# Local attention without the row maximum, with each head's transposed part issued one head later

## The reference

```python
q = q.reshape(Bq * h, nb, window, d) * scale          # window 128, d 64
kk = look_around(k); vv = look_around(v)              # 3 blocks = 384 keys
sim = jnp.einsum('bnid,bnjd->bnij', q, kk)
sim = jnp.where(valid, sim, neg)                      # keys beyond either end of the sequence
attn = jax.nn.softmax(sim, axis=-1)
out = jnp.einsum('bnij,bnjd->bnid', attn, vv)
```

## Time and profile before

| | us |
|---|---|
| median of the two timed runs | 4406.5 (4383.72 and 4429.28) |
| the profiled execution | 4304.85 |
| its span, first to last instruction, slowest core (core 7) | 4303.3 |
| spans of the eight cores | 4293.8 to 4303.3 |
| mean granted TensorE clock of the cores (1 is full speed) | 0.709 to 0.711 |

### The profile page before, as it was taken

One profiled execution on the slowest core, in us unless ns is written; L12 is line 12 of the kernel. 1 busy time (PEld: TensorE's weight loads), 2 busy tenths in 40 slices (PEclk: granted clock), 3 DMA queues, 4 the chain that ended last, 5 costly groups with the idle time before them and its releaser, 6 DMA issues.

```text
span 4303.3 us, 34639 instructions; the slowest of 8 cores (4293.8 to 4303.3 us)
## 1 busy us (share of the span) xinstructions
PE 1987.4 (46%) x10661; PEld 955.0 (22%) x10661; DVE 993.4 (23%) x2186; ACT 898.7 (21%) x1889; POOL 34.9 (1%) x68
## 2 busy tenths in 40 slices
PE   1223455434334333433334678683011566666666
PEld 0011122211111111111112455451001222222222
DVE  2243322122222222222232211212234111011111
ACT  0122322222222222222210222321012111111111
POOL 0000000000000000000011000000000000000000
PEclk9566777655555555555566889896555799999999
DMA  7311111301100100010046110103621000000000
GB/s 236 116 58 60 65 59 54 103 30 44 35 25 30 54 25 25 30 44 25 10 144 195 59 48 30 54 20 95 183 98 59 32 25 13 25 25 25 25 25 10
DMA packets 107777, 249.52 MB, mean 58 GB/s; under 512 B 29865, under 2 KB 44337, under 8 KB 105550
## 3 DMA queue, kind: packets, MB, share of 16 engines
q1 hardware_dynamic: 74544, 170.20, 12.9%
q10 hardware_dynamic: 27938, 60.33, 3.6%
q0 software_dynamic: 5120, 16.78, 1.1%
HBM read 186.95 MB, written 60.32 MB: 57 GB/s over the span
## 4 chain that ended last, share of the span: by engine, by line
PE 41%; DVE 18%; ACT 16%; issue 11%; DMA 11%; ACTq 1%; DVEq 1%; SPq 0%; PEldq 0%; PEld 0%; POOLq 0%
PE bank L1513 6%; PE bank L1479 5%; PE bank L1134 4%; PE bank L1113 4%; ACT arena L850 4%; DMA arena<-w_in 4%; DVE arena L844 3%; PE bank L651 3%; DMA arena<-wfc2T 3%; ACT arena L866 3%; PE bank L860 3%; PE bank L839 2%; PE bank L834 2%; PE bank L911 2%; PE bank L876 2%
## 5 line engine op out<-in xcount | busy, mean ns | idle before, releaser
L860 PE MATMUL bank<-ident_bf,arena 128*128 128x128 bf16 x768 | 122.5, 296 | 563.7 <-ACT arena L850 563.7
L1134 PE MATMUL bank<-arena 128*128 128x256 bf16 x2048 | 287.3, 288 | 175.5 <-DVE arena L1047 99.2
L1513 PE MATMUL bank<-arena 128*128 128x512 bf16 x1024 | 269.0, 410 | 109.1 <-ACT arena L1504 109.1
L844 DVE TENSOR_REDUCE arena<-bank 128x1 f32<-128x384 f32 x256 | 142.4, 556 | 613.7 <-PE bank L839 613.7
L1113 PE MATMUL bank<-arena 128*128 128x512 bf16 x1024 | 268.8, 386 | 9.7 <-ACT arena L1142 9.7
L1134 PEld LDWEIGHTS bank<-arena 128*128 128x128 bf16 x2048 | 209.7, 103 | 265.5 <-issue 184.6
L850 ACT ACTIVATE arena<-bank,arena 128x384 bf16<-128x384 f32 x256 | 148.7, 581 | 568.1 <-DVE arena L844 568.1
L1479 PE MATMUL bank<-arena 128*128 128x512 bf16 x1024 | 245.7, 383 | 3.2 <-DMA arena<-s_h2T 3.2
L1492 DVE TENSOR_SCALAR arena<-arena 128x512 bf16<-128x512 f32 x128 | 62.2, 486 | 772.2 <-ACT arena L1488 772.2
L860 PEld LDWEIGHTS bank<-ident_bf,arena 128*128 128x128 bf16 x768 | 61.6, 119 | 656.2 <-issue 656.2
L1142 ACT ACTIVATE arena<-bank,arena 128x256 bf16<-128x256 f32 x256 | 120.8, 475 | 411.6 <-PE bank L1134 411.5
(11 more groups left out here) (162 smaller groups left out, 2244.1 us busy)
## 6 DMA issues: line engine op xcount, KB each, us to landing
arena<-wmod SPq DMA_DIRECT2D x16, 1536.0 KB, 8.2
arena<-x_ext SPq DMA_DIRECT2D x34, 512.0 KB, 5.2
arena<-wfc2T POOLq DMA_DIRECT2D x64, 256.0 KB, 4.4
arena<-wfc1T SPq DMA_DIRECT2D x64, 256.0 KB, 4.2
arena<-w_in SPq DMA_DIRECT2D x64, 256.0 KB, 2.7
arena<-w_in SPq DMA_DIRECT2D x32, 512.0 KB, 4.4
arena<-s_s SPq DMA_DIRECT2D x32, 512.0 KB, 5.0
arena<-wqkvT SPq DMA_DIRECT2D x16, 768.0 KB, 5.7
```

Of the source, the lines that this page charges most:

```text
L844: E.op("vector", lambda e, b=scb, hh=h: e.reduce_max(negmax[:, hh:hh + 1], bf(b)[:, 0:WIN], axis=AX.X, negate=True), inc=SMX.bump())
L860: E.op("tensor", lambda e, jj=j, pp=p_sb[idx % 2]: e.transpose(bb(2)[:, jj * 128:(jj + 1) * 128], pp[:, jj * 128:(jj + 1) * 128], ident_bf ...
L1134: e.matmul(bf(b)[:, 0:256], wfc1_bf[:, kk * DFF + mm * 128: kk * DFF + mm * 128 + 128], zt[:, kk * 256:(kk + 1) * 256], start=(kk == 0), s ...
L1513: b=obks[n]: e.matmul(bf(b)[:, :], tT_bf[ii % 2][:, ts(kk, 128)], w2_bf[:, (ee * 4 + kk) * 1024 + nn * 512: (ee * 4 + kk) * 1024 + nn * 51 ...
```

## The change

It does five things, all in the attention stage.

1. The row maximum is gone: line 844, negmax and the semaphore SMX. ACT waits for the scores (SSC) itself, and Exp is given no bias.
2. The mask matmul is issued only in tiles 0 and 15. In the other 14 the third score matmul closes the group and raises SSC.
3. The transposes, the copy to pT_sb and the value matmuls of a head are put in a function, emit_ptv, which is called for head h-1 behind head h's scores, Exp and reciprocal; the last head's is called after the loop. Within a tile the streams read: PE scores(h), transposes(h-1), values(h-1), scores(h+1); ACT Exp(h), Exp(h+1); DVE reciprocal(h), copy(h-1), reciprocal(h+1).
4. The copy to pT_sb is done by DVE (tensor_copy), no longer by ACT. The normalizations of a half stand in emit_ptv, behind its last head's value matmuls.
5. The waits of PE for the tile's values ("vv") stand ahead of the tile's first scores, with those for the keys.

```diff
--- before.py
+++ after.py
@@ -733,7 +733,6 @@
     x1_sb = [A.alloc(f"x1sb{i}", [128, D], F32) for i in range(2)]
     sxa_sb = [A.alloc(f"sxasb{i}", [128, D], F32) for i in range(2)]
     sxa_t1 = A.alloc("sxa_t1", [128, D], F32)
-    negmax = A.alloc("negmax", [128, HEADS], F32)
     ssum = A.alloc("ssum", [128, HEADS], F32)
     rrb = A.alloc("rrb", [128, HEADS], F32)
     sq_tr2 = A.alloc("sq_tr2", [128, D], F32)
@@ -746,7 +745,6 @@
     LHs = [mkdma(f"LH{i}") for i in range(2)]
     LX2s = [mkdma(f"LX2{i}") for i in range(2)]
     SSC = mksem("SSC")
-    SMX = mksem("SMX")
     SEXP = mksem("SEXP")
     SRR = mksem("SRR")
     SPT = mksem("SPT")
@@ -817,79 +815,84 @@
 
         qg = q_ring[g % 4]
         qcol0 = (t % 4) * 128
+        masked = t in (0, NT_OWN - 1)
+
+        def emit_ptv(idx):
+            hh = idx % HEADS
+            tt = idx // HEADS
+            hf = hh // 8
+            so = hh % 8
+            waitr("tensor", SEXP, idx + 1)
+            waitr("tensor", SPTE, idx)
+            for j in range(3):
+                E.op("tensor", lambda e, jj=j, pp=p_sb[idx % 2]: e.transpose(
+                    bb(2)[:, jj * 128:(jj + 1) * 128],
+                    pp[:, jj * 128:(jj + 1) * 128], ident_bf[:, :]),
+                    inc=SPT.bump() if j == 2 else None)
+            E.wait("vector", SPT, SPT.n)
+            waitr("vector", SVM2, idx - 1)
+            E.op("vector", lambda e, pt=pT_sb[idx % 2]: e.tensor_copy(
+                pt[:, :], bb(2)[:, 0:WIN]), inc=SPTE.bump())
+            E.wait("tensor", SPTE, SPTE.n)
+            if so == 0:
+                waitr("tensor", SOEV, 8 * ((tt * 2 + hf) - 1))
+            for j in range(3):
+                E.op("tensor", lambda e, jj=j, sl=(tt + j) % 4, h2=hh, hf2=hf,
+                     pt=pT_sb[idx % 2]: e.matmul(
+                         bf(3 + hf2)[:, (h2 % 8) * 64:((h2 % 8) + 1) * 64],
+                         pt[:, jj * 128:(jj + 1) * 128],
+                         v_ring[sl][:, h2 * 64:(h2 + 1) * 64],
+                         start=(jj == 0), stop=(jj == 2)),
+                     inc=SVM2.bump() if j == 2 else None)
+            if so == 7:
+                E.wait("vector", SVM2, SVM2.n)
+                E.wait("vector", SRR, SRR.n)
+                if tt > 0 and hf == 0:
+                    waitr("vector", SAOT, tt)
+                    wdma("vector", ("dbgao", tt - 1))
+                for h2i in range(hf * 8, hf * 8 + 8):
+                    E.op("vector", lambda e, hh2=h2i, hf2=hf: e.tensor_scalar(
+                        ao_sb[:, hh2 * 64:(hh2 + 1) * 64],
+                        bf(3 + hf2)[:, (hh2 % 8) * 64:((hh2 % 8) + 1) * 64],
+                        rrb[:, hh2:hh2 + 1], None, ALU.mult),
+                        inc=SOEV.bump())
+
         for h in range(HEADS):
             idx = t * HEADS + h
-            half = h // 8
-            slot = h % 8
             plane = h // 2
             prow = (h % 2) * 64
             scb = idx % 2
             if h == 0:
                 for w in range(3):
                     wdma("tensor", ("kv", t + w))
+                    wdma("tensor", ("vv", t + w))
                 wdma("tensor", ("qg", g))
             waitr("tensor", SEXP, idx - 1)
             for j in range(3):
                 E.op("tensor", lambda e, jj=j, sl=(t + j) % 4, b=scb, pl=plane,
-                     pr=prow, q0=qcol0, qgb=qg: e.matmul(
+                     pr=prow, q0=qcol0, qgb=qg, mk=masked: e.matmul(
                          bf(b)[:, jj * 128:(jj + 1) * 128],
                          qgb[pr:pr + 64, pl * 512 + q0: pl * 512 + q0 + 128],
                          k_ring[sl][pr:pr + 64, pl * 128:(pl + 1) * 128],
-                         start=(jj == 0), stop=False))
-            E.op("tensor", lambda e, b=scb, tt=t: e.matmul(
-                bf(b)[:, 0:WIN], ones_bf[0:1, 0:128],
-                maskrow_bf[0:1, tt * WIN:(tt + 1) * WIN],
-                start=False, stop=True), inc=SSC.bump())
-            E.wait("vector", SSC, SSC.n)
-            E.op("vector", lambda e, b=scb, hh=h: e.reduce_max(
-                negmax[:, hh:hh + 1], bf(b)[:, 0:WIN], axis=AX.X, negate=True),
-                inc=SMX.bump())
-            E.wait("scalar", SMX, SMX.n)
+                         start=(jj == 0), stop=(jj == 2 and not mk)),
+                     inc=SSC.bump() if (j == 2 and not masked) else None)
+            if masked:
+                E.op("tensor", lambda e, b=scb, tt=t: e.matmul(
+                    bf(b)[:, 0:WIN], ones_bf[0:1, 0:128],
+                    maskrow_bf[0:1, tt * WIN:(tt + 1) * WIN],
+                    start=False, stop=True), inc=SSC.bump())
+            E.wait("scalar", SSC, SSC.n)
             waitr("scalar", SPT, idx - 1)
             E.op("scalar", lambda e, b=scb, hh=h, pp=p_sb[idx % 2]:
                  e.activation(pp[:, :], bf(b)[:, 0:WIN], AF.Exp,
-                              bias=negmax[:, hh:hh + 1],
                               accum_out=ssum[:, hh:hh + 1]), inc=SEXP.bump())
             E.wait("vector", SEXP, SEXP.n)
             E.op("vector", lambda e, hh=h: e.reciprocal(rrb[:, hh:hh + 1],
                                                         ssum[:, hh:hh + 1]),
                  inc=SRR.bump())
-            E.wait("tensor", SEXP, SEXP.n)
-            waitr("tensor", SPTE, idx)
-            for j in range(3):
-                E.op("tensor", lambda e, jj=j, pp=p_sb[idx % 2]: e.transpose(
-                    bb(2)[:, jj * 128:(jj + 1) * 128],
-                    pp[:, jj * 128:(jj + 1) * 128], ident_bf[:, :]),
-                    inc=SPT.bump() if j == 2 else None)
-            E.wait("scalar", SPT, SPT.n)
-            waitr("scalar", SVM2, idx - 1)
-            E.op("scalar", lambda e, pt=pT_sb[idx % 2]: e.activation(
-                pt[:, :], bb(2)[:, 0:WIN], AF.Copy), inc=SPTE.bump())
-            E.wait("tensor", SPTE, SPTE.n)
-            if h == 0:
-                for w in range(3):
-                    wdma("tensor", ("vv", t + w))
-            if slot == 0:
-                waitr("tensor", SOEV, 8 * ((t * 2 + half) - 1))
-            for j in range(3):
-                E.op("tensor", lambda e, jj=j, sl=(t + j) % 4, hh=h, hf=half,
-                     so=slot, pt=pT_sb[idx % 2]: e.matmul(
-                         bf(3 + hf)[:, so * 64:(so + 1) * 64],
-                         pt[:, jj * 128:(jj + 1) * 128],
-                         v_ring[sl][:, hh * 64:(hh + 1) * 64],
-                         start=(jj == 0), stop=(jj == 2)),
-                     inc=SVM2.bump() if j == 2 else None)
-            if slot == 7:
-                E.wait("vector", SVM2, SVM2.n)
-                E.wait("vector", SRR, SRR.n)
-                if t > 0 and half == 0:
-                    waitr("vector", SAOT, t)
-                    wdma("vector", ("dbgao", t - 1))
-                for h2i in range(half * 8, half * 8 + 8):
-                    E.op("vector", lambda e, hh=h2i, hf=half: e.tensor_scalar(
-                        ao_sb[:, hh * 64:(hh + 1) * 64],
-                        bf(3 + hf)[:, (hh % 8) * 64:((hh % 8) + 1) * 64],
-                        rrb[:, hh:hh + 1], None, ALU.mult), inc=SOEV.bump())
+            if h > 0:
+                emit_ptv(idx - 1)
+        emit_ptv(t * HEADS + HEADS - 1)
         if "s_dbgao" in taps:
             E.wait("scalar", SOEV, SOEV.n)
             dma("scalar", lambda e, tt=t: e.dma_start(
```

## The result

| | kernel before | changed kernel |
|---|---|---|
| median, us | 4341.85 (10 runs, 4301.69 to 4462.11) | 3822.9 (12 runs, 3815.65 to 3999.45) |
| profiled execution, us | 4304.85 | 3827.66 |
| attention stage: first scores to start of the last projection | 810.9 to 2163.5, 1353 us | 812.8 to about 1682, 869 us |

The ratio of the times is 0.885, with a 95% interval of 0.881 to 0.888: 11.5% faster. In some executions of either kernel the cores of one die, or of both, show a lower granted clock and take some per cent longer; the ratios here leave those out, the medians and ranges do not. The stages around the attention stage kept their length: 811 and 813 us up to the first scores, and 2140 and 2144 us from the start of the last projection to the end of the span (4303.3 - 2163.5; 3825.3 - 1681.7).

The account below looks back on a forecast made before the run. Bound by a latency chain across engines in the attention stage: 31.8 us a tile, 509 in all, less 14 and 1, saves 494 of 4304.85, giving 3811 us; 3860 stated, between that and 3880 to 3920 for timed runs; range 3740 to 3980.

Parts of the forecast that it names:

- The bound: Attention stage: a chain of latencies, with PE, DVE and ACT each busy 24 to 39% and no engine full.
- The closed chain of the new turn: Head loop: scores, Exp, reciprocal, copy, values still form one closed chain; a turn of 2.22 us, 1.96 less than 4.18.
- The copy's start behind the reciprocal: DVE in a turn: reciprocal to start of the copy 0.13 us, bounds 0.08 and 0.29.
- The middle of a tile: Behind the normalizations, the reciprocal late by 0.5 us plus one more PE wait: 0.6 us, for 0.8 before.
- The tile's end: Tile boundary: scores(15) to values(15) 3.47 us; next scores to first Exp 7.43; from there to scores(2) 2.3.
- The projection: Between a tile's last values and the next tile's scores: 10.47 us, carried over as before.
- What was costed at nothing: PE's earlier waits for values, SP's loads, transfers and stages outside: hidden or untouched; the values' waits, if uncovered, 0.3 us a tile.
- From the profiled execution to the stated time: Whole kernel: 3811 us by profile, 3880 to 3920 if timed runs lie as far above theirs; 3860 stated between.
- The clock in the head loop: Rival, PE in the head loop: clock rises from 1.2 to 2.4 GHz, 3724 us by the profiled execution; chance 0.12.
- The bounds' case: Rival, head-loop turn: all terms at upper bounds, 0.66 us a turn, 169 us more, 3980 us; chance 0.14.
- The transposes are hidden: Turn: transposes off the chain, 0.35 us slack; rival: they return, turn 2.22 + 0.74, 4001 us, chance 0.05.
- No table was loaded: Rival, ACT around each Exp: two table loads a head, 2.57 us, making it 156 us slower, 4461 us; chance 0.01.

## Why the prediction was right

The stated 3860 us lies 1% above the 3823 measured and the range holds it. The mechanism is the one forecast; how near the sum came is in part luck, since some errors of its terms cancel. By its steps:

- **The bound.** Right. A chain of latencies through three engines, none of them full; what was cut from the chain came off the time, part by part.
- **The closed chain of the new turn.** Right: 2.22 forecast, 2.25 measured. Its terms, from the timeline above: scores to Exp 0.65 (0.65), Exp to the end of the sum 0.58 (0.58), to DVE 0.10 (0.11), reciprocal to copy 0.17 (0.13), copy 0.36 (0.36), to PE 0.15 (0.14), values to scores 0.24 (0.25), the forecast in brackets. The Exp without bias costs what the copy on ACT did, so the 0.09 was the bias and not the row sum; with the maximum put back, the Exp with bias and sum takes 0.58 again, which shows it from the other side. By the Trainium skill, "ScalarE: Activation LUTs", section "What ACT_TABLE_LOAD costs", it would be 506 ns, an estimate; the trace has 491.
- **The copy's start behind the reciprocal.** This term was mis-sized, by 0.04. I took the row of two DVE operations that overlap; in a turn the copy starts 0.01 after the reciprocal's end. The Trainium skill, "VectorE: DVE Perf Modes", section "The DRAIN you can't avoid", would have had it so, though the same section lets an operation that is not held start earlier. With the reciprocal behind the copy it starts 0.09 before the copy's end (1307.74 for 1307.83). And in the middle of a tile of the changed kernel the very same pair overlaps: the copy starts at 1328.34, 0.08 before the reciprocal's end (1328.27 + 0.15), in the rows below. So the kind of operation does not decide it. Where two overlap, the second has one wait (here, and in the earlier trace rows) or DVE had been busy with the normalizations for 1.63 us ahead; where they do not, the copy has two waits, and DVE had been idle for 1.73 us up to the reciprocal of 0.16. That waits are got through while the engine is still busy, and two of them take longer than that reciprocal, fits all of these places, but no run tests it.
- **The middle of a tile.** 0.6 forecast; the turn there is 1329.18 - 1326.41 = 2.77, 0.52 above the others, the reciprocal standing behind the normalizations (line 854). The timeline of the middle and the end of a tile of the changed kernel, the answer to the earlier trace rows:

```profile
1326.41 0.50 PE L873 MATMUL bank<-arena 64*128 64x128 bf16 x3
1326.72 1.63 DVE L854 TENSOR_SCALAR arena<-bank,arena 128x64 bf16<-128x64 f32 x8 [0.71 <-PE bank L841]
...
1328.27 0.15 DVE L890 RECIPROCAL arena<-arena 128x1 f32<-128x1 f32 x1
1328.34 0.34 DVE L834 COPY arena<-bank 128x384 bf16<-128x384 bf16 x1
...
1329.18 0.50 PE L873 MATMUL bank<-arena 64*128 64x128 bf16 x3
...
1340.45 0.50 PE L873 MATMUL bank<-arena 64*128 64x128 bf16 x3
...
1343.84 0.32 PE L841 MATMUL bank<-arena 128*128 128x64 bf16 x3 [0.68 <-DVE arena L834]
```

- **The tile's end.** From scores(15) to values(15) 3.47 forecast, 1343.84 - 1340.45 = 3.39 measured, in the last two of those rows; from the next scores to the first Exp 7.43 and 1308.29 - 1300.88 = 7.41; from there to scores(2) 2.3 and 1310.63 - 1308.29 = 2.34, in these rows:

```profile
1300.88 0.35 PE L873 MATMUL bank<-arena 64*128 64x128 bf16 x6
...
1308.15 0.20 ACT L264 ACTIVATE stats_ln<-arena 128x1 f32<-128x1 f32 x1
1308.29 0.49 ACT L887 ACTIVATE arena<-bank 128x384 bf16<-128x384 f32 x1
...
1310.63 0.50 PE L873 MATMUL bank<-arena 64*128 64x128 bf16 x3
```

- **The projection.** Wrong: 10.47 us were carried over "as before", 11.56 came. The instructions were unchanged and their price was not, because the clock rose later after their start. It makes about 1 us in most tiles, 12 in all, and is most of why a tile takes 54.4 us and not 53.2; the turn's 0.03 makes another 0.4. The stage shrank by 1353 - 869 = 484 us where the sum had 494. It would have been further off if the sum had not also come out 0.4 us short for the tile before (84.97 for 85.4), 7 us in all, which nobody planned.
- **The mask.** Right: 0.43 a head, 0.44 where it was put back.
- **What was costed at nothing.** Right: the other stages kept their lengths, no load became late, and no line of the stage in the changed kernel waits for a DMA but the first scores.
- **From the profiled execution to the stated time.** The sum gave 3811 by the profiled execution, 0.3% below the 3822.9 measured and 17 us below the profiled execution of the changed kernel; 10 of these lie in the stage and 6 in the stages around it. I then went half way to the two timed runs known by then, 1.8 and 2.9% above their profile. This was the larger error, 49 us: both of those two lie above seven of the eight executions that were timed later (4301.69 to 4381.68).
- **The rivals.** The clock in the head loop stayed at 1.2 GHz, and did so even where PE is shown busy without a gap. The bounds' case did not come; no term came near its upper bound. The transposes are hidden, with 0.57 us to spare for 0.35 forecast: they start 0.43 behind the scores, so the two waits that I had added there cost nothing. No table was loaded in the stage.

What the prediction did not ask is whether each part helps. It priced the copy on DVE at 0.36 and never compared it with leaving it on ACT in the same order, where the same terms give 2.05 for 2.22, nor with the reciprocal one place later.

## What to carry to other kernels

When heads or tiles overlap in software, write down for each in-order stream what stands ahead of the instruction that releases the next turn: the slowest thing ahead of it sets the turn, even if it is a small one that waits on something this turn does not need (0.16 us of reciprocal, waiting for the Exp, held a copy back by 0.39 us, in 12 of the 16 turns of every tile). A latency taken off a closed chain comes off once per turn whatever the engines' busy shares say; a faster engine for an instruction is worth having only if that engine's stream lets it start as early. And a price carried over as unchanged is safe only while the clock it was read at is.

## What the runs showed of the hardware that I had not expected

- TensorE's granted clock stayed at 0.50 while PE showed matmuls without a gap for 8 us (turns of scores on 64 rows, transposes, and values of 64 columns; 960 columns in 1.03 us), and rose to 1.00 in a projection of 512-column matmuls on 128 rows, one every 0.427 us. Writing the transposes as plain matmuls changed neither the clock nor the turn.
- The same 16 matmuls of a projection took from 5.3 to 6.9 us, as the clock rose 2.6 to 6.0 us behind their start; of an extra 1.14 us ahead of them 0.5 was paid on average, and next to nothing in some tiles.
- Two DVE operations in a row overlapped by 0.08 to 0.09 us where the second had one wait, long met (copy, then reciprocal), and also with two (reciprocal, then copy) in the middle of a tile, where DVE had been busy for 1.63 us ahead. In a normal turn the same copy, behind a reciprocal that DVE had sat idle for, began 0.01 us after its end.
